# Inverse slot sums at the front of a batch's last group, and a drain group that goes tile by tile in halves

## The reference

```
x = _layernorm(x, norm_g, norm_b)
se = _layernorm(slot_embeds, slot_g, slot_b) * scale
logits = jnp.einsum('bnd,esd->bnes', x, se)
dispatch = jax.nn.softmax(logits, axis=1)
combine = jax.nn.softmax(logits.reshape(x.shape[0], x.shape[1], -1), axis=-1)
slots = jnp.einsum('bnd,bnes->besd', x, dispatch)
gate = jax.nn.gelu(jnp.einsum('besd,edf->besf', slots, Wg) + bg[None, :, None, :], approximate=False)
up = jnp.einsum('besd,edf->besf', slots, Wu) + bu[None, :, None, :]
eout = jnp.einsum('besf,efo->beso', gate * up, Wd) + bd[None, :, None, :]
return jnp.einsum('bns,bso->bno', combine, eout)
```

## Time and profile before

| | |
|---|---|
| median of three executions | 1861.09 us |
| lowest and highest | 1861.06 and 1861.68 us |
| the profiled execution | 1854.48 us |
| its span | 1852.8 us |
| busy share of the span | PE 97%, weight loads 87%, DVE 71%, ACT 63%, POOL 45% |
| granted clock of TensorE, mean | 0.998 |
| f1 route stage: `inverse_sums` | 171.2 to 446.2 us, four times |
| f2 route stage: `inverse_sums` | 1214.5 to 1488.6 us, four times |

### The profile page before, as it was taken

The page is one execution under the profiler, slowest core; times in us unless marked ns, Lnnn a source line. Parts: engine busy times, 40 slices in busy tenths (PEclk is TensorE's granted clock), DMA queues, the critical chain, the costliest instruction groups (busy, mean ns, idle before and its releaser), DMA issues. The chain is left out here.

```text
span 1852.8 us, 35562 instructions
## 1 busy us (share of the span) xinstructions
PE 1800.0 (97%) x11756; PEld 1620.4 (87%) x11756; DVE 1309.5 (71%) x2365; ACT 1161.3 (63%) x2285; POOL 825.1 (45%) x1036
## 2 busy tenths in 40 slices
PE   6999999999999999999999999999999999999998
PEld 5788888878999999989999877888888789999998
DVE  6866666664899888855555587666565668997886
ACT  5776676675665777754444367666666755667774
POOL 3423334234788655422222134242432458885553
PEclk9999999999999999999999999999999999999999
DMA  4642443251654777712222165333323426647773
GB/s 156 233 151 100 159 158 119 108 192 36 221 195 156 254 268 267 285 47 69 68 68 68 58 238 193 120 142 147 148 102 114 159 88 230 204 173 269 262 257 146
DMA packets 106940, 297.85 MB, mean 161 GB/s; under 512 B 16784, under 2 KB 56592, under 8 KB 94544
## 3 DMA queue, kind: packets, MB, share of 16 engines
q1 hardware_dynamic: 106832, 296.49, 44.7%
HBM read 187.18 MB, written 109.28 MB: 160 GB/s over the span
## 5 line engine op out<-in xcount | busy, mean ns | idle before, releaser
L115 POOL TENSOR_TENSOR pool_carrier<-minus_half 128x1 f32<-128x1 f32 x224 | 71.7, 320 | 599.5 <-PE f2bank L984 197.6
L824 ACT ACTIVATE f2r_lt<-f2bank,slot_shift 128x512 f32<-128x512 f32 x128 | 88.3, 690 | 125.3 <-PE f2bank L955 125.2
L824 ACT ACTIVATE f1r_lt<-f1bank,slot_shift 128x512 f32<-128x512 f32 x128 | 88.3, 690 | 122.1 <-PE f1bank L955 122.0
L673 DVE TENSOR_TENSOR f2r_e_lo<-f2bank,f2r_e_hi 128x512 fp32r<-128x512 f32 x128 | 82.4, 685 | 80.6 <-ACT f2r_e_hi L905 80.6
L673 DVE TENSOR_TENSOR f1r_e_lo<-f1bank,f1r_e_hi 128x512 fp32r<-128x512 f32 x128 | 82.4, 684 | 79.7 <-ACT f1r_e_hi L905 79.7
L1685 PE MATMUL f1bank<-f1c_eo,f1c_e_hi 128*128 128x258 f32 (+1 forms) x512 | 130.6, 287 | 0.5 <-DVE f1c_xout L1591 0.4
L1685 PE MATMUL f2bank<-f2c_eo,f2c_e_hi 128*128 128x258 f32 (+1 forms) x512 | 130.0, 286 | 0.5 <-DVE f2c_xout L1591 0.4
L1686 PE MATMUL f1bank<-f1c_eo,f1c_e_hi 128*128 128x256 f32 (+1 forms) x512 | 128.2, 282 | 0.0
L1686 PE MATMUL f2bank<-f2c_eo,f2c_e_hi 128*128 128x256 f32 (+1 forms) x512 | 128.1, 282 | 0.0
L1538 POOL TENSOR_TENSOR f1c_e_lo<-f1c_lt,f1c_e_hi 128x512 fp32r<-128x512 f32 x64 | 82.7, 1294 | 76.7 <-ACT f1c_e_hi L1651 76.7
L1538 POOL TENSOR_TENSOR f2c_e_lo<-f2c_lt,f2c_e_hi 128x512 fp32r<-128x512 f32 x64 | 82.8, 1295 | 75.7 <-ACT f2c_e_hi L1651 75.7
(11 more groups left out here) (347 smaller groups left out, 6661.2 us busy)
## 6 DMA issues: line engine op xcount, KB each, us to landing
logits<-f1r_lt SPq DMA_DIRECT2D x16, 2048.0 KB, 7.3
f1c_lt<-logits SPq DMA_DIRECT2D x32, 1024.0 KB, 7.3
logits<-f2r_lt SPq DMA_DIRECT2D x16, 2048.0 KB, 7.3
f2c_lt<-logits SPq DMA_DIRECT2D x32, 1024.0 KB, 7.0
normalized<-t_xin SPq DMA_DIRECT2D x32, 512.0 KB, 2.6
t_xin<-in_L_attn_x SPq DMA_DIRECT2D x16, 512.0 KB, 5.1
f1r_xback<-normalized SPq DMA_DIRECT2D x16, 512.0 KB, 8.1
f1e_raw_g<-in_L_ffn_Wg SPq DMA_DIRECT2D x16, 512.0 KB, 3.9
```

The lines of the kernel that those rows point to most:

```text
L115: pool.tensor_tensor(c["pool_carrier"][:, col:col + 1], c["minus_half"][:, 0:1], c["minus_half"][:, 0:1], ALU.add)
L673: dve.tensor_tensor(e_lo[t % 2][:, h * BANK:(h + 1) * BANK], ps_t[h][:, :], rd(e_hi[t % 2][:, h * BANK:(h + 1) * BANK]), ALU.subtract).the ...
L824: act.activation(lt[:, g, sc, :], ps_l[sc % 2][:, :], ACT.Identity, bias=c["slot_shift"][:, sc:sc + 1]).then_inc(logit_out, 1)
```

## The change

In fill and drain steps, `inverse_sums(b, j)` moves on DVE from behind e_lo of tile 1 to behind the token statistics, ahead of the group's first maximum. This holds for steps 1 to 3 of both feed-forwards; in step 4 it stays. On PE, tiles 1 and 2 of group 0 of step 4 no longer transpose both halves of the next tile and then dispatch both of their own: each half of transposes is followed by the same half of matmuls, and each waits only for its half of e_lo.

```diff
@@ -729,6 +729,8 @@
                     exp_lo(j, 0, 1)
                 if nxt2:
                     token_stats(i + 2, g % 2)
+                if drain and fill and g == NG - 1:
+                    inverse_sums(b, j)
                 over_tokens(0)
                 if fill and not drain and g >= 2:
                     behind(2)
@@ -748,8 +750,6 @@
                     dve.wait_ge(row_tr, 1 + B * NG)
                     dve.wait_ge(logit_mm, NSC * B * NG)
                     experts.first_gate_up(dve)
-                if drain and fill and g == NG - 1:
-                    inverse_sums(b, j)
                 if fill and g == NG - 1:
                     negative_max(b, i, j, 0, drain)
                 if fill:
@@ -1058,6 +1058,14 @@
                             transpose_exp(j, g, 1, False, (h,))
                         pe.wait_ge(logit_out, NSC * B * NG)
                         transpose_row_max(i - 2, row_bank(*group_behind(b, g, 2)))
+                    elif drain and not fill and g == 0 and t < GT - 1:
+
+                        for h in range(HB):
+                            pe.wait_ge(e_lo_done, 1 + HB * (GT * j + t) + h + 1)
+                            transpose_exp(j, g, t + 1, False, (h,))
+                            if h == 0:
+                                pe.wait_ge(xs_done, 1 + GT * j + t + 1)
+                            dispatch_half(b, g, j, t, h)
                     elif drain:
                         if not (not fill and g == NG - 1 and t == GT - 1):
                             pe.wait_ge(e_lo_done, 1 + HB * (GT * j + t + 1))
```

## The result

The changed kernel takes 1854.44 us (median of 17 executions, 1851.90 to 1860.85), the kernel before in the same comparison 1860.70 us (17 executions, 1855.41 to 1863.59). The ratio is 0.9972, with a 95% interval of 0.9965 to 0.9980: 0.28% faster, or 5.2 us, with 3.7 to 6.5 us by the interval; the two medians lie 6.3 us apart. The forecast was 5.3 us less and 1855.8 us.

What follows compares the result with a forecast made beforehand. PE, busy 97% of the span, was taken as the bound, so time comes only from its waits. Early inverses 3.78 us plus halves 1.51 us make 5.29, from 1861.09 to 1855.8 us; own range 1855.0 to 1857.2.

Steps and rivals of the forecast that it cites:

- third rival: More than forecast: some waits left standing go too and the step 3 chain is shorter; 1854.6 us, chance 0.03.
- the outer range: 1854.4 to 1859.0 us for the whole kernel, leaving out the two long DMA chain cases.
- Step 1 of the feed-forwards, 1.56 + 0.24 us: After step 1, early inverses end PE's stop before token transposes L942, gaining 1.56 us in f1, 0.24 in f2.
- 7.5 us to spare: In step 1, the load of the inverses lands at 178.6, while L787 has to start by 186.1.
- The second rival: DMA chain from inverse store to L787 stretches: about 24 us gives 1859.2, chance 0.08; 25 gives 1865.2, 0.04 for 25+.
- Step 3, 0.82 + 1.16 us: L787 waits for PE's half 0, not DMA; step 4's first matmul comes 0.82 us earlier in f1, 1.16 in f2.
- The halves, 0.75 + 0.76 us: Tiles 1 and 2, group 0 of step 4: halves gain 0.75 us in f1 and 0.76 in f2.
- the split: Doing a tile's transposes and matmuls in halves was to cost PE 0.18 us for each of two tiles.
- The 0.11 us: At tile 3, e_lo comes at 416.34 while PE is free at 416.23, so it is late by 0.11 us.
- "The second step of either feed-forward has nothing to give.": After step 2 the distance on PE was already 9.72 us, so early inverses gain nothing there.
- the places are bound by the order of engines that run alike: Reason for taking the same 5.3 us gain from the median as from the profiled execution.
- "What comes later in the program keeps its pace.": Behind the routes nothing is lost: the expert stage starts from PE's last dispatch.

Runs made afterwards that it cites:

- the two other comparisons: Changed kernel, word for word, measured again beside the kernel before on two other chips: 1854.61 us, ratio 0.9949, and 1854.68 us, ratio 0.9973.
- the last chip: Chip that ran the kernel before once more, and early inverse sums with or without halves and the second logits load later; ratios 0.9998 to 0.9916.
- the row maxima first: Changed kernel with PE's row-maxima transposes ahead of tile 0's matmuls in step 4: 1857.48 us, ratio 0.9965 to the kernel before.
- before again: Kernel before, word for word, measured and profiled a second time on another chip: 1866.51 us, ratio 0.9998 to the kernel before.
- halves alone: Kernel before with only PE's halves in step 4, inverse sums in the old place: 1861.88 us, ratio 0.9988.
- the inverses alone: Kernel before with only the inverse sums moved early, no halves: 1858.34 us, ratio 0.9972; on another chip 1857.47 us, ratio 0.9944.
- the logits apart: Changed kernel with the combine's second logits load one expert pair later: 1852.38 us, ratio 0.9960, then 1851.42, 0.9916; without halves 1853.37, 0.9926.

## Why the prediction was right, and where not

**The forecast.** 1855.8 us and 5.3 us less, 0.71 for faster; measured 1854.44 us and 5.2 us less by the ratio. The time lies below the forecast's own range (1855.0 to 1857.2), where the prediction had its third rival (1854.6), and a few hundredths inside the outer range (1854.4 to 1859.0). The routes of the two profiles differ by 5.11 us, so the places and the sum are right for this pair of profiles. That the ratio of the executions comes within 0.1 us of that sum is in part luck: the two other comparisons of the same kernels gave 9.5 and 5.0 us, and what the inverses earn differs from profile to profile, as told below.

**Step 1 of the feed-forwards, 1.56 + 0.24 us.** The store was expected at 162.54 and goes at 164.80; f1's route starts 2.19 us later in this profile, so it is in its place. L942 is dense and the distance 9.72 us in both feed-forwards, a gain of 1.56 and 0.24, as forecast. The 7.5 us to spare shrank, since the store takes 11.2 to 13.4 us, but L787 starts 9.6 us after the load's issue where the load needs 5.1, so 4.5 us are left by these rows. On the last chip the store took up to 14.7 us, with 8.3 us to L787; 3 us are left there. The second rival, a chain of 24 us, was never near: the longest is 14.71 us plus a load of some 5.

**Step 3, 0.82 + 1.16 us.** L982 came out at 1.06 and 1.03 us behind the transposes, where the forecast had 0.98; the gain is 0.74 and 1.11 us. The size was off by 0.08 in f1 and 0.05 in f2, and the term is the start of L787: the prediction had it 1.17 us ahead of the transposes (402.25 against 403.42), and it starts 1.09 us ahead in f1 (403.03 against 404.12) and 1.12 us in f2. The chain behind it is as forecast.

**The halves, 0.75 + 0.76 us.** The group stretch is 12.94 and 12.91 us, where 12.92 was forecast. Taking the first gain off, the halves give 0.81 us in f1 and 0.82 in f2. One term was mis-sized: the split costs 0.12 us a tile, not 0.18. The 0.11 us that were to be late at tile 3 have no wait of their own in these rows, though the transposes at 417.06 start 0.42 us behind the last matmul (416.64), where a dense stream has 0.23: about 0.2 us stay there. The run with the row maxima first shows that an earlier start of this order brings no more, since e_lo is then late.

**"The second step of either feed-forward has nothing to give."** This step failed. It was read from one profile, in which the load of the inverses landed just in time after step 2. The same trace shows how near that was. L787 waited for the DMA there too:

```profile
296.01 2.73 DVE L787 SCALAR_TENSOR_TENSOR f1r_slots<-f1bank,gain,f1r_inv_rows 128x512 f32 x4 [2.77 <-DMA f1r_inv_rows<-inverse]
```

From the store to L787 it took 14.52 us. The distance is 4.7 to 4.9 us shorter than this chain wherever it is longer than 9.72, so a chain of more than about 14.5 us lengthens it, and with 14.52 us (14.43 in f2) there was next to no slack. In three profiles with the old place (before, before again, halves alone) the distance there was 9.72, 10.22 and 10.07 us in f1, and 9.72, 10.26 and 9.96 in f2. The same holds for my sentence that the places are bound by the order of engines that run alike. It is true of the wait of 0.98 us ahead of tile 2's transposes, which all ten feed-forwards without the halves have; the others end with a DMA, and are worth 3.6 us in one profile and 7.2 in the next. The two profiles come from different comparisons, so it is not shown how much differs between executions of one chip and how much between chips. The speed of the execution is no guide to it: the first profile is of one that stood 6.6 us under the median, the second of the fastest of its twelve, 4.8 us under the median, and it lost twice as much. Measured, the two parts are worth 0.28%, 0.51% and 0.27% in three comparisons, and the inverses alone 0.28% and 0.56%, where 3.78 us would be 0.20%.

**"What comes later in the program keeps its pace."** No single profile can show it: without the logits apart, the experts scatter by 3.3 us in f1 and 3.6 in f2 over the profiles, and the stretch of attention by 4.4 with the clock. In the three comparisons both parts bring 5.2, 9.5 and 5.0 us, where the two routes of the first pair are shorter by 5.1 us, so the times show no loss behind the routes.

## What to carry to other kernels

A wait that ends with a DMA had no one size here: take its price from several profiles, or from the landing times' spread, and treat a place where the DMA is now just in time as one that will be late in other executions. The wait that ended with an engine's order came back to the hundredth of a microsecond, and was forecast by walking the chain. Where an urgent DMA can be issued earlier at no cost to its engine, do it even if the profile at hand shows no wait, and look next for the large transfers that are issued ahead of urgent ones, as the logits here.

## What the hardware showed that I had not expected

A store of 1024 values of 4 bytes takes 8.5 to 11.7 us in one place and 11.1 to 14.7 in another, of which the 512 KB load issued 0.4 us ahead of it makes about 1 us. The store takes 14.0 to 14.7 us after step 1 of f1 in the three profiles of one chip with the early place, and 12.6 to 13.8 us in the six on the two other chips of the experiments.

After a stop of PE of 2 to 3 us the granted clock can fall to half, behind the restart and not in the stop in the rows below. In the profile of the halves alone, f2, after a wait of 1.94 us at 1456.11 (length, busy us and instructions, granted clock, DMA share, GB/s):

```profile
1450.00:1457.00 7.00, 5.06 (x27) 1.00 1.00 321
1457.00:1460.20 3.20, 3.20 (x12) 0.50 0.94 384
1460.20:1465.00 4.80, 4.80 (x30) 0.98 1.06 374
```

0.50 is the lower of the clock's two levels, 1.2 GHz of 2.4. A matmul of the route is 0.63 us long there instead of 0.39, and the "group" stretch of that f2 is 1.5 us longer than in its f1 when the "first" stretch is taken off both (15.92 - 2.54 against 13.95 - 2.06). The expert stage of the changed kernel has the same behind its 2.97 us:

```profile
1562.00:1566.00 4.00, 1.03 (x9) 1.00 0.66 230
1566.00:1570.00 4.00, 4.00 (x23) 0.57 0.33 66
...
1575.00:1590.00 15.00, 15.00 (x127) 1.00 0.35 114
```

It is not certain to happen: after the 2.44 us at 1452.40 of the second profile of before, the clock stayed at 1.00 (1452.4 to 1460), and behind the stop of 2.9 us near 810, which every profile has, it stayed at 1.00 in five, fell for about 3 us in three and for about 6 us in six. The stretch of combine and attention around it takes 488.0, 489.9 and 491.3 us on the mean of the three kinds. What decides between them was not settled.
